# Attention's first loads put one by one behind stores, modulation rows loaded behind stores too, and a last sum taken over by the matmul engine

## What is computed

```python
x = L0_attn_x
mod = (_silu(L0_c) @ L0_wmod).reshape(L0_c.shape[0], 6, 1, -1)
sa, ca, ga, sb, cb, gb = (mod[:, 0], mod[:, 1], mod[:, 2], mod[:, 3], mod[:, 4], mod[:, 5])
h = _layernorm(x, axis=-1) * (1 + ca) + sa
x = x + ga * attention(h)      # causal, 16 heads of 32
h = _layernorm(x, axis=-1) * (1 + cb) + sb
x = x + gb * ffn(h)            # 4 of 32 experts of width 256, and a shared one of width 1024
```

## Time and profile before

| | us |
|---|---|
| median of three runs | 3142.4 |
| lowest and highest | 3134.63, 3147.78 |
| the profiled execution | 3153.8 |
| its span, first to last instruction | 3152.0 |
| PE busy | 2934.1 (93%) |
| mean granted clock of PE | 0.968 of full |

### The profile page before, as it was taken

How to read it: one execution, slowest core, us unless ns; L and a number is a source line. 1 busy time by engine, 2 the same in 40 slices (tenths; PEclk the granted TensorE clock), 3 DMA queues, 4 the chain that set the end, 5 groups by cost and what they waited for, 6 DMA issues and landing times. The chain is left out here.

```text
span 3152.0 us, 49674 instructions
## 1 busy us (share of the span) xinstructions
PE 2934.1 (93%) x16384; PEld 2169.5 (69%) x16384; DVE 2113.4 (67%) x5338; ACT 1341.7 (43%) x2435; POOL 1876.1 (60%) x1099
## 2 busy tenths in 40 slices
PE   7999999899999999999999389999999999947997
PEld 5788888666666665666665268888887877736775
DVE  6555555577777777777774457888887778736774
ACT  2222222156666665666666233323323322316774
POOL 1332223178788877887888344576667657545564
PEclk9999999999999999999999689999999999978998
DMA  6555556645645654565452332333233232108996
GB/s 228 205 197 189 177 184 190 187 108 132 139 111 116 137 129 110 116 136 130 110 129 50 111 124 95 95 103 98 86 107 103 77 95 93 57 15 258 229 233 132
DMA packets 281371, 419.46 MB, mean 133 GB/s; under 512 B 48399, under 2 KB 132623, under 8 KB 281166
## 3 DMA queue, kind: packets, MB, share of 16 engines
q1 hardware_dynamic: 258638, 383.17, 42.8%
q0 software_dynamic: 22528, 33.72, 5.6%
HBM read 262.33 MB, written 153.01 MB: 132 GB/s over the span
## 5 line engine op out<-in xcount | busy, mean ns | idle before, releaser
L140 DVE CUSTOM_DVE_ANT_0 att_ps_s<-att_ps_s,att_causal 128x512 f32<-128x512 f32 (+1 forms) x992 | 470.7, 504 | 195.6 <-PE att_ps_s L983 195.2
L911 ACT ACTIVATE att_pt<-att_ps_p 128x512 f32<-128x512 f32 (+1 forms) x1024 | 526.1, 588 | 139.3 <-PE att_ps_p L1031 103.1
L983 PE MATMUL att_ps_s<-att_ks,att_qs 96*128 96x512 f32 x1488 | 514.7, 373 | 7.3 <-PEq L210 3.7
L1028 PE MATMUL att_ps_p<-att_qs,att_ks 98*128 98x512 f32 (+3 forms) x1536 | 506.0, 370 | 7.7 <-ACT att_pt L911 7.1
L861 POOL TENSOR_TENSOR att_gathered<-att_gathered,att_pt 128x2048 f32<-128x2048 f32 (+1 forms) x96 | 405.3, 4222 | 41.8 <-ACT att_pt L911 36.8
L854 POOL TENSOR_TENSOR att_pt<-att_pt 128x1024 f32<-128x1024 f32 (+2 forms) x160 | 345.4, 2159 | 74.8 <-PE att_ps_o L993 49.3
L146 DVE TENSOR_REDUCE att_lower<-att_ps_s 128x1 f32<-128x512 f32 x496 | 340.0, 685 | 71.5 <-PE att_ps_s L983 71.5
L1028 PEld LDWEIGHTS att_ps_p<-att_qs,att_ks 98*128 98x128 f32 x1536 | 272.6, 191 | 154.9 <-issue 106.8
L1306 POOL DMA_INDIRECT slot_info<-ffn_info,ffn_slot x256 | 272.7, 1065 | 123.5 <-issue 78.8
L983 PEld LDWEIGHTS att_ps_s<-att_ks,att_qs 96*128 96x128 f32 x1488 | 276.8, 191 | 81.0 <-DVE att_rowmax L140 23.8
L384 POOL TENSOR_TENSOR qkv_x<-qkv_x,qkv_mod 128x512 f32<-128x512 f32 x60 | 83.5, 1391 | 383.9 <-DVE qkv_x L474 383.9
(11 more groups left out here) (290 smaller groups left out, 6836.4 us busy)
## 6 DMA issues: line engine op xcount, KB each, us to landing
att_qs<-qk_parts SPq DMA_DIRECT2D x96, 512.0 KB, 6.9
att_ks<-qk_parts SPq DMA_DIRECT2D x96, 512.0 KB, 12.8
qk_parts<-qkv_out_hi SPq DMA_DIRECT2D x128, 256.0 KB, 2.6
qk_parts<-qkv_out_lo SPq DMA_DIRECT2D x128, 256.0 KB, 2.9
qkv_x<-x SPq DMA_DIRECT2D x16, 1024.0 KB, 5.7
v_rows<-qkv_out_v SPq DMA_DIRECT2D x64, 256.0 KB, 2.3
att_vs<-v_rows SPq DMA_DIRECT2D x32, 512.0 KB, 16.1
o_parts<-att_o SPq DMA_DIRECT2D x64, 256.0 KB, 6.3
```

What stands on the lines that cost most here:

```text
L140: dve.tensor_tensor_reduce(part, part, self.causal[:, UNIT - (c1 - c0):UNIT], scale=1.0, scalar=MASKED, op0=ALU.add, op1=ALU.max, accum_ou ...
L911: act.activation(tile(c)[:, h, col:UNIT], ps_p[(NPROB * prev.g + n) % NP][:, col:UNIT], ACT.Exp, scale=float(HD) ** -0.5).then_inc(exp_don ...
L983: pe.matmul(bank("s", cur.g, i)[:, 0:c1 - c0], qs[cur.slot][0:STACK, h, t * P:(t + 1) * P], ks[cur.slot][0:STACK, h, c0:c1], start=True, s ...
L1028: last = pe.matmul(part[:, i * (UNIT - col):(i + 1) * (UNIT - col)], ks[prev.slot][:, h + i, kt * P:(kt + 1) * P], qs[prev.slot][:, h + i, ...
```

## The change

Three things. SP's loads of attention's groups 0 and 1 are no longer issued in one go. A new `load_part` issues one of the seven, and in the last batch SP issues one behind each of the first seven pairs of stores: group 0 in unit 14, group 1 (all seven) in unit 15. The load of the modulation rows, with its wait for POOL, stands behind the eight pairs of stores instead of ahead of them. And for the last group of attention POOL leaves out the joins of chunks 10, 11 and 9; PE sums those tiles itself in `total`. The other groups are as before (`load` in attention issues the same seven loads in the same order).

```diff
@@ class Bridge
-    def load_heads(self, sp, g, slot, q, k, v, qk_dram, v_dram, keys=True, rest=True):
+    def load_part(self, sp, n, g, slot, q, k, v, qk_dram, v_dram):
+        if n < 6:
+            tile, part = (q, k)[n // 3], ((QHI, QHI, QLO), (KHI, KLO, KHI))[n // 3][n % 3]
+            src = qk_dram[part, bass.ds(g, 1), :, :].rearrange("o (h d) t -> d (o h) t", d=HD)
+            sp.dma_start(raw(tile[n % 3 * HD:(n % 3 + 1) * HD, :, :]), src).then_inc(self.q_in[slot], 16)
+        else:
             src = v_dram[bass.ds(g, 1), :, :].rearrange("o (k p) j -> p (o k) j", p=P)
             sp.dma_start(v[:, :, :], src).then_inc(self.v_in[slot], 16)
@@ stage_modulate_qkv, sync, body
-                    bridge.load_heads(sp, 0, 0, bridge.qs[0], bridge.ks[0], bridge.vs[0], qk_dram, v_dram)
-                    bridge.load_heads(sp, 1, 1, bridge.qs[1], bridge.ks[1], bridge.vs[1], qk_dram, v_dram, keys=False)
                 if not more:
                     sp.wait_ge(tr_done, CREDIT + DK * NB * HALVES)
-                    bridge.load_heads(sp, 1, 1, bridge.qs[1], bridge.ks[1], bridge.vs[1], qk_dram, v_dram, rest=False)
                 if more or half == 0:
                     if not isinstance(b, int) or b < LAST:
                         sp.wait_ge(tr_done, CREDIT + DK * (u + 1))
                         load_x(b + 1, half)
-                        if half == 0:
-                            sp.wait_ge(h_done, CREDIT + UT * (u + 2))
-                            if isinstance(b, int) and b == 0:
-                                sp.wait_ge(rows_out, 32)
-                            load_mod(b + 1)
                 for n in range(NQK):
 ...
+                    if isinstance(b, int) and b == LAST and n < 7:
+                        bridge.load_part(sp, n, half, half, bridge.qs[half], bridge.ks[half], bridge.vs[half], qk_dram, v_dram)
+                if half == 0 and (not isinstance(b, int) or b < LAST):
+                    sp.wait_ge(h_done, CREDIT + UT * (u + 2))
+                    if isinstance(b, int) and b == 0:
+                        sp.wait_ge(rows_out, 32)
+                    load_mod(b + 1)
@@ stage_attention
+        ALONE = (10, 11, 9)
@@ gpsimd, step
                     for c in JOINS:
-                        join(prev, c)
+                        if cur or c not in ALONE:
+                            join(prev, c)
@@ tensor
-            def total(group, qh):
+            def total(group, qh, alone=()):
                 bank_free("sum", group.g, qh)
-                pe.wait_ge(add_done, CREDIT + NJ * group.g + JOINED[qh])
-                for part in ([tile(0)], [gathered, tile(6)])[qh]:
+                pe.wait_ge(add_done, CREDIT + NJ * group.g + JOINED[qh] - len(alone))
+                parts = ([(tile(0), 0)], [(gathered, 0), (tile(6), 0)])[qh] + [(tile(c), span(c)) for c in alone]
+                for n, (part, col) in enumerate(parts):
                     for h in range(GH):
-                        last = pe.matmul(bank("sum", group.g, qh)[h * HD:(h + 1) * HD, :], ones[:, :], part[:, h, :],
-                                         start=part is not tile(6), stop=part is not gathered)
+                        last = pe.matmul(bank("sum", group.g, qh)[h * HD:(h + 1) * HD, col:UNIT], ones[:, :], part[:, h, col:UNIT],
+                                         start=n == 0, stop=n + 1 == len(parts))
@@
-            total(end, 1)
+            total(end, 1, ALONE)
```

More of the change, by code:

```diff
@@ L789, in load @@
             def load(G):
-                bridge.load_heads(sp, G.g, G.slot, qs[G.slot], ks[G.slot], vs[G.slot], qk_dram, v_dram)
+                for n in range(7):
+                    bridge.load_part(sp, n, G.g, G.slot, qs[G.slot], ks[G.slot], vs[G.slot], qk_dram, v_dram)
             def store(group, qh):
```

## The result

The changed kernel took 3102.7 us (median of four runs, 3095.0 to 3108.0), against 3141.7 us for the kernel before (median of four). The ratio is 0.987, with an interval of 0.9849 to 0.9891: 34 to 47 us less. The forecast was 27 us less and a range that begins at 3104, so the direction was right, the size too small, and the median lies 1.3 us outside the range.

What follows compares the result with a forecast made beforehand. PE, busy 93% of the span, was taken as the bound, so only its waits pay: 8.9 (modulation rows) + 12.3 (unit 14) - 0.7 + 6.5 (end) = 27.0 us, median 3142.4 to 3115, range 3104 to 3131.

Steps and rivals of the forecast that it cites:

- the 3.24 us of unit 0: PE's wait in unit 0 for the modulation rows, which moving their load behind the stores would remove: 3.24 us gained.
- That gives 5.7 us: First halves of the loop's units would run like second halves, removing six PE waits: 5.7 us gained.
- Unit 14: Unit 14 without the block of eleven loads takes 34.8 us instead of 47.13: 12.3 us gained, less 0.7 for thin margin.
- The step was 3.46 us and not 3.67: SP queue in unit 14: one load (2.36 us) plus one pair of stores (1.31 us) was taken to cost 3.67 us.
- the margin: Group 0's sixth load known at 34.4 us into unit 14, unit 15 starting at 34.8: 0.4 us to spare.
- The 0.7 us put aside for a late group 0: Deduction of 0.7 us from unit 14's gain, because group 0's loads complete barely before unit 15's first score.
- Unit 15 at no cost: Unit 15 gets seven loads instead of three; the queue keeps up at 3.99 us a result: cost 0.
- The end, 6.5: End of attention: PE no longer waits for POOL's last join, and ACT's copy starts 6.5 us earlier.
- Late group 0: Rival, 3123 us: mixed steps cost up to 4.7 us, PE waits at unit 15's start, clock falls; chance 0.19.
- Little from the modulation rows: Rival, 3121 to 3124 us: PE waits for the next late thing where the 0.95 us stood; chance 0.06.
- The end doesn't do it: Rival, 3121.5 us: PE's last sum is held by its bank or the copy, 6.5 us not gained; chance 0.05.
- SP held at every load: Rival, 3190 us: each load step holds SP about 9 us in units 14 and 15, 48 us slower; chance 0.03.

## Why the prediction was right or wrong

**The sum was 27.0, and the parts measure 34.** By the profiles with and without each edit: unit 0 8.2 (a mean of six against 38.5), the loop 7.0, unit 14 11.6 (46.3 as the mean of seven profiles, 34.7 as the mean of five), the end 7.0. The four measurements of the whole change's gain, 41 in the first pair (34 to 47), 35.5 on chip A (30 to 41), 43 on C (36 to 49) and 32 on D (28 to 37), lie around that.

**The step that failed: "the 3.24 us of unit 0".** The mechanism was right, the term was mis-sized: the edit alone in unit 0 gained 9.7 us (6 to 13), and by the profiles 8.2. I took the length of a wait from one execution, in which PE happened to arrive late at it. It also lacked what comes behind a wait: in the usual execution PE works at the lower clock after it. With 8.2 in place of 3.24 the forecast would have been 3110, and the lower end of the range, worked out in the same way, 3099. Of the 12 us between the forecast 27 and the 39 between the medians, 5.0 are this term, 1.3 the loop (below), 0.5 the end, and some 5 stand in no part that the edits touch. That rest is within the interval (34 to 47); its cause stays open.

**The loop, "That gives 5.7 us", was 1.3 short.** A clean unit is 34.57 us. I had worked it out as 34.8 from unit 2 less its wait, though the second halves show it directly: from 148.90 on the earlier trace rows to the next unit. A difference of unit lengths holds what a row of waits leaves out.

**Unit 14 was right in its mechanism, and in its exact number partly by luck.** 11.6 was taken and 11.6 measured. The step was 3.46 us and not 3.67; the first store, the margin and the ordering of events came as worked out. Result 7 was evicted 1.3 us later than I had it, and ACT waited 3.72 us for a store where I had said under 3, which PE did not feel. The 0.7 us put aside for a late group 0 were not needed; unit 14 had been some 0.8 us longer in the first profile than in the mean of seven, and the two cancel. Most of the care went into fitting the loads between the stores, and that is the part worth under 1 us. The rule of the Trainium skill ("DMA: Bandwidth & Descriptors", section "Rules for kernel authors") that a transfer be issued early and waited for late did not decide. The later issue left no wait at all. On this queue, which also carries the stores, early loads delayed them: ACT waited 20.23 us behind eleven, 9.92 behind seven, and at most 3.72 with one between two pairs.

**Unit 15 at no cost was right**, 50.1 us in all pairs; its pace was (591.60 - 563.68) / 7 = 3.99 us a result, as before. **The end, 6.5, was right**: 6.9 and 7.0, the copy 3.78 us after the last weighing, within the 3.5 to 4.3 stated.

**The rivals.** Late group 0: falls, by 0.7 us of margin. Little from the modulation rows: falls, the reverse is true. The end doesn't do it: falls. SP held at every load: falls. In unit 14 SP was held twice, for the 3.48 us of the last store shown and for 4.80 us at the four stores of v, with nothing urgent behind either. One slip of arithmetic: a third of the rivals' 0.30, and the 0.04, give faster 0.83, same 0.14 and slower 0.03, not 0.81, 0.15 and 0.04.

**What stays open.** Why PE begins unit 0 at the lower clock in some executions. And why the gain was 43 us on chip C, with 34 in the parts, and 32 on chip D. The excess stands where the third stage is long and stalls, and in single profiles of chip A the stage was shorter with the end edited (1049 and 1050 us) than without (1057 and 1062), and ACT's waits called remote were there 30.7 and 25.2 us without it and none with it. The medians of chip A leave little room for such an effect: the end alone gained 8.5 us (4 to 14), of which 7.0 are the end itself. On chips B and D nothing of the kind is seen. No run had the kernel before profiled on chip C, so a small effect of the change on these stalls is neither shown nor excluded.

## What to carry to other kernels

A wait in a profile has a beginning and an end, set by two different engines. Before its length is booked as a gain, ask whether its beginning was typical in this execution (here the clock at the start of the stage said that it wasn't), and measure the stretch from mark to mark against a clean one, since slower work after the wait belongs to it.

On a queue that carries both stores someone waits for and loads nobody wants yet, first take out the loads that have another place, and only then think of spreading the rest.

Compare profiles of two kernels only stage by stage, and only on one chip, before a difference in a stage that the edit doesn't touch is explained.

## What was not expected of the hardware

The length of one stage that no edit touches went with the chip: 1028 to 1029 us in all traces of two of them, 1049 to 1062 on a third, 1086 and 1090 on the fourth, and with it the median of the kernel before, 3114 to 3183 us, 2.2%. Within a chip the runs agree far better, and the ratio of the whole change was 0.987 to 0.990 in all four measurements.

A queue that alternates loads into 32 partitions with stores from 128 took 3.46 us for 1 MB, which is 303 GB/s, above the 286 that the two rates of the earlier trace rows give in turn (1048576 bytes in 3.67 us). The Trainium skill ("SBUF — State Buffer", section "Door 1: The DMA port swizzle") gives 32 partitions half of the ports and an asymptote of some 218 GB/s. The trace agrees: while only q and k loads were served, before the change, the queue moved 216 GB/s, and the 222 of the earlier trace rows have a load of v in them:

```profile
538.00:554.00 16.00, 16.00 (x72) 13.24 (x71) 8.58 (x21) 2.86 (x5) 11.45 (x12) 1.00 1.03 216
```

That a store may use the other half beside a load is only argued; no run tested it.
